# Attention on one core: a piece of V's products moved between a slot's two pairs of score products

## The reference, cut to what matters

```python
b, s, e = x.shape                      # 8, 512, 256
h = rel_table.shape[1]                 # 16
scale = e ** (-0.5)
q = split_heads(x @ Wq)
k = split_heads(x @ Wk)
v = split_heads(x @ Wv)
attn = jnp.einsum('bhqd,bhkd->bhqk', q, k) * scale
attn = jax.nn.softmax(attn, axis=-1)
attn = attn + bias[None]               # from rel_table
out = jnp.einsum('bhqk,bhkd->bhqd', attn, v)
out = out.transpose(0, 2, 1, 3).reshape(b, s, e)
mu = jnp.mean(out, axis=-1, keepdims=True)
var = jnp.var(out, axis=-1, keepdims=True)
out = (out - mu) / jnp.sqrt(var + EPS) * gamma + beta
```

## Time and profile before

| | us |
|---|---|
| runs shown | 1941.26, 1942.33, 1943.03 (median 1942.33) |
| profiled execution, its own time | 1946.43 |
| its span | 1944.7 |
| the attention loop in it (first to last transposed score product) | 862.8 to 1256.5 |

### The profile page before, as it was taken

One profiled execution on the slowest core, in us unless ns is written; L12 is line 12 of the kernel. 1 busy time (PEld: TensorE's weight loads), 2 busy tenths in 40 slices (PEclk: granted clock), 3 DMA queues, 4 the chain that ended last, 5 costly groups with the idle time before them and its releaser, 6 DMA issues. The chain is left out here.

```text
span 1944.7 us, 33241 instructions
## 1 busy us (share of the span) xinstructions
PE 1649.3 (85%) x9891; PEld 1115.5 (57%) x9892; DVE 1146.3 (59%) x1949; ACT 1080.2 (56%) x2236; POOL 659.6 (34%) x624
## 2 busy tenths in 40 slices
PE   4999999561599689899999999945999999999990
PEld 1433343260499656444444444433999999999990
DVE  6999998388411174358999999366233333333325
ACT  6888987540133234127788888625455555555554
POOL 0000000030266331211233333211576777777750
PEclk9999999775699889989999999985999999999995
DMA  5000000134122196603333434069344444444417
GB/s 179 1 0 1 0 1 0 47 103 157 33 67 64 47 336 234 111 1 78 78 100 100 100 100 111 24 211 335 53 70 71 70 69 71 65 68 70 69 21 259
DMA packets 145735, 173.67 MB, mean 89 GB/s; under 512 B 29139, under 2 KB 110430, under 8 KB 145504
## 3 DMA queue, kind: packets, MB, share of 16 engines
q1 hardware_dynamic: 104160, 128.29, 21.7%
q0 software_dynamic: 33248, 43.71, 12.7%
q10 hardware_dynamic: 8224, 0.39, 0.2%
HBM read 111.50 MB, written 66.19 MB: 91 GB/s over the span
## 5 line engine op out<-in xcount | busy, mean ns | idle before, releaser
L1359 PEld LDWEIGHTS f_ht_ps<-f_XT,f_WS 128*128 128x128 f32 x2912 | 358.6, 195 | 15.1 <-DVE f_WS L1452 2.6
L1359 PE MATMUL f_ht_ps<-f_XT,f_WS 128*128 128x128 f32 x2912 | 361.7, 278 | 3.0 <-ACT f_XT L1400 3.0
L1367 PE MATMUL f_y_ps<-W,f_HT 128*128 x1456 | 344.3, 380 | 0.0
L1325 POOL DMA_INDIRECT moe<-f_Y,TOK x182 | 276.9, 1521 | 185.3 <-ACT f_Y L1425 142.2
L2187 DVE TENSOR_REDUCE att_MX<-att_s_ps 128x2 f32<-128x1024 f32 x256 | 304.3, 1215 | 53.6 <-PE att_s_ps L1951 53.4
L2152 ACT ACTIVATE att_PT<-att_st_ps 128x512 f32<-128x512 f32 x512 | 278.7, 594 | 69.8 <-PE att_st_ps L1976 59.6
L1367 PEld LDWEIGHTS f_y_ps<-W,f_HT 128*128 128x128 f32 x1456 | 263.0, 191 | 28.2
L1452 DVE COPY f_WS<-W 128x1024 f32 x182 | 134.0, 737 | 205.0 <-PE f_ht_ps L1359 124.8
L1316 POOL DMA_INDIRECT XG<-x,TOK x182 | 191.1, 1050 | 178.6 <-issue 108.5
L1460 DVE TENSOR_TENSOR f_Y<-f_y_ps,f_B 128x256 f32<-128x256 f32 x143 | 60.7, 424 | 296.4 <-PE f_y_ps L1367 296.4
L303 PE MATMUL rec_ring<-rec_XC,rec_W 128*128 128x512 f32 x384 | 182.9, 630 | 49.7 <-DVE rec_XC L353 21.1
(11 more groups left out here) (291 smaller groups left out, 2191.3 us busy)
## 6 DMA issues: line engine op xcount, KB each, us to landing
W<-in_w SPq DMA_DIRECT2D x48, 512.0 KB, 10.0
att_Q<-qk_pairs SPq DMA_DIRECT2D x192, 64.0 KB, 2.8
att_K<-qk_pairs SPq DMA_DIRECT2D x192, 64.0 KB, 2.9
qk_pairs<-prj_HI SPq DMA_DIRECT2D x16, 512.0 KB, 3.8
qk_pairs<-prj_LO SPq DMA_DIRECT2D x16, 512.0 KB, 5.1
hidden<-in_xT SPq DMA_DIRECT2D x8, 512.0 KB, 7.7
x<-n_Y SPq DMA_DIRECT2D x8, 512.0 KB, 3.0
prj_X<-x SPq DMA_DIRECT2D x8, 512.0 KB, 8.8
```

Source lines behind the costliest of these rows:

```text
L1325: nc.gpsimd.indirect_dma_start(out=outs[n % len(outs)], out_offset=bass.IndirectOffsetOnAxis(ap=TOK[:, n:n + 1], axis=0), in_=Y[n % R][:], ...
L1359: mm = nc.tensor.matmul(ht_ps[r % 2][:, f * P:(f + 1) * P], WS[r % 2][:, at:at + P], XT[r % 2][:, c], start=(c == 0), stop=(c == DC - 1))
L1367: mm = nc.tensor.matmul(y_ps[r % 2][:], HT[r % 2][:, f], W2[:, bass.ds(e * W_EXPERT + f * D, D)], start=(f == 0), stop=(f == FC - 1))
```

## The change

In the slot, `sums` moves ahead of the second pair. Nothing is added or removed, and no wait is changed:

```diff
@@ -2059,11 +2059,11 @@
                     scores_T(i, slot, 0)
                     if i + LEAD < TWO:
                         scores(i + LEAD, slot, 1)
+                    if n >= 1:
+                        sums(n - 1, at)
                     if i + LEAD < TWO:
                         scores(i + LEAD, slot, 0)
                     scores_T(i, slot, 1)
-                    if n >= 1:
-                        sums(n - 1, at)
                     if p == 0 and slot == 1 and n + 1 < NGROUPS:
                         maxima(n + 1)
                     if p == 0 and slot == 3 and n >= 2:
```

## The result

The changed kernel takes 2011.35 us (median of four runs, 2009.39 to 2015.58) against 1942.68 before: a ratio of 1.0357, 95% interval 1.0340 to 1.0375. The direction was forecast, the size was not: +69 us in place of +40, outside the range of 1954 to 2002.

A forecast was written before the change was run, and what follows sets the result against it. PE was taken to set the pace, DVE having only 7% of air. +35.0 us for groups 2 to 29, 1.7 aggregates, 0.8 group 1 and 2 groups 30 and 31 made +39.5: median 1982, range 1954 to 2002.

The forecast's parts named there:

- PE's own work: PE's queue in each slot: plain slots still cost 1.22 us, slot 1 1.84 as before, slot 3 1.98, 0.06 less.
- the removed wait: Fourth product's weight load waiting for ACT's exponential: this wait, about 0.2 us in slot 5 and in slot 7, disappears.
- rival C: Slightly slower: only additional drain and load exposure in slots 1 and 3 count, 0.2 each, +12 us, 1954; chance 0.09.
- The first pair directly behind a second pair: PE at the slot's border: spacing without a wait taken as 0.34 us, bounds worth -8 and +17 us in total.
- ACT's side: Later second exponential delays the next slot's first; the old wait returns at the first product, two slots costing 2.65 us.
- DVE's side: Later reductions free buffers late: second product 0.12 us late in slot 6, 0.43 in slot 7; slots become 1.44 and 1.75.
- The group's border: V's piece 0 waits for slot 7's late exponential and ACT's copy, starting at 1.31; slot 0 2.21 us against 1.43.
- The sum of a group: Changes of slots 0 to 7 add to +1.25 us per group, +35.0 over the 28 groups 2 to 29.
- the 0 taken for the stall: POOL's residual holding DVE's CAST of slot 7 in six groups: difference taken as 0, bounds -1 and +1.2 us per group.
- Groups 1, 30 and 31 at full clock: Group 1 waits for exponentials but no copy, +0.8 us; groups 30 and 31 keep the border's wait, +2.
- the granted clock is 0.99, its level of 2.4 GHz: Clock read in the loop's stretch from 876.3 to 1228.3 us before the change; no forecast term changed it.
- PE's busy time in the loop: Sign to look for in the changed kernel's profile: the same or less, with more idle before it.

The follow-up runs named there:

- e12: Changed kernel with ACT's exponentials computing 256 of 512 columns from group 2 on; 2041.62 us, ratio 1.0490.
- e4: Changed kernel with DVE doing scale ahead of slot 4's reduction; four runs of 1984.35 to 2032.18 us, no ratio.
- e1: Changed kernel with V's piece between the pairs in slots 1 to 6 only, behind both pairs in slots 0 and 7; 1972.23 us, ratio 1.0161.
- e5: Changed kernel with ACT's copy of the sums between slot 7's two exponentials, not behind both; 1995.40 us, ratio 1.0257.
- e7: Changed kernel with six dummy transposes in slot 0's idle spot, plus eight small products per slot of group 0; 1988.50 us, ratio 1.0223.
- e8: Kernel before the change, with eight added products of 128 columns in each slot of group 0; 1944.24 us, ratio 1.0002.
- e3: Changed kernel with six dummy transposes on PE between slot 0's first pair and V's piece; 1986.08 us, ratio 1.0220.
- e14: Changed kernel with 256-column exponentials from group 2 on and six dummy transposes in slot 0's idle spot; 1980.91 us, ratio 1.0194.
- e10: Kernel before the change, with ACT copying the sums twice before releasing PE, except in the last three groups; 1953.26 us, ratio 1.0052.
- e13: Kernel before the change, with ACT copying the sums three times before releasing PE, except in the last three groups; 1974.12 us, ratio 1.0161.

## Why the prediction was wrong, by its own steps

**PE's own work and the removed wait**: right but for slot 2. Plain slots that nothing delays are 1.32 to 1.33, the fourth product no longer waits in full-clock slots, and in slots 1 and 3 nothing of rival C's 0.2 is seen (1.84 and 1.90, against 1.86 and 2.05 before). The first pair directly behind a second pair, which no row had shown, starts 0.34 later where nothing holds it; the value taken was right. Slot 2 is 0.11 longer than the 1.22 I gave it: its first product is not loaded ahead (it follows the maxima), which I had counted in slot 4 and forgot here. Slot 3 is 0.08 shorter than I gave it, as its first product is loaded ahead.

**ACT's side**: right. Slot 5 is 1.37 against 1.33, and 1.22 with short exponentials (e12): the wait did come back as one of the first product.

**DVE's side**: right. Slots 6 and 7 are 1.43 and 1.76 against 1.44 and 1.75, and e4 shows that scale between two reductions is the cause in slot 7. For slot 6, which e4 left at 1.43, the cause is the trace's releaser (DVE's reduction); no run tests it.

**The group's border**: right in mechanism, 0.13 too small. V's piece starts at 1.45 of slot 0, not 1.31: from the copy's end to its first matmul 0.14 pass (1050.86 to 1051.00), where I had taken 0.04, which is 0.10 of it. e1 and e5 show that slot 7's late exponential and the copy behind it make the wait.

**The sum of a group**: 1.37 as a mean, against 1.25 and the aggregates' 0.06: 38 against 37 us for groups 2 to 29, right. Groups with the aggregates grew by 1.67 (forecast 1.54), those with the residual by 1.12 (1.25 with the 0 taken for the stall).

**Groups 1, 30 and 31 at full clock**: nearly right. Where both orders run group 1 at 2.4 GHz, it takes 11.87 (e7) against 11.17 (e8), +0.70 for a forecast of +0.8. Groups 30 and 31 take 30.8 us at full clock (e3) against 27.7, +3.1 for a forecast of +2. With groups 2 to 29 that makes 42 us for the order alone, and the forecast had 39.5.

**What failed** is the step "the granted clock is 0.99, its level of 2.4 GHz": I kept it, and so a price of nothing for the clock, for a kernel in which I forecast an idle spot of about 1 us per group and two smaller ones. None of my terms nor rivals had the clock. In its place the profile shows 88 us of the loop at 1.2 GHz, against 17 before, and some 25 of the 67 us by which the loop grew are the price: 3.3 in group 1 (4.0 less the order's 0.7), 13.2 in groups 27 and 28, and 8.5 in groups 30 and 31 (11.6 less 3.1). Two pairs of runs show that it is the clock: e3, whose slots are the same, lost 25 of the 69 us by keeping PE busy, and the same fill took 61 us from e12 (e14). e3, which keeps 2.4 GHz from group 2 on, is the run to hold my sum against: 1986, 4 above it.

One of my signs failed too: PE's busy time in the loop was to be the same or less, and rose from 384.7 to 426.2 us. A product that takes 0.49 to 0.50 at 2.4 GHz takes 0.79 at 1.2. Not all of it is the clock: by the stretches of 330 us at full clock PE is busy for 12.4 us per group, against 11.9 before.

What a low stretch costs comes from the changed kernel: groups 27 and 28 lose 13.2 us over 37.5 at 1.2 GHz, 0.35 for each. A plain slot takes 2.13 there, with PE hardly idle (below, the second pairs of two slots in a row):

```profile
1239.85 0.79 PE L1951 MATMUL att_s_ps<-att_K,att_Q 48*128 48x512 f32 x1
...
1241.98 0.79 PE L1951 MATMUL att_s_ps<-att_K,att_Q 48*128 48x512 f32 x1
```

Open stays what exactly starts a fall and what ends it. In the changed kernel the clock fell at the start of group 27, but group 14 has the same idle spots as group 26 (1.05 and 0.31), and nothing happens behind it. e4 and e10 have idle spots of one size and differ. And the changed order stayed at 1.2 GHz for 37.5 us with PE busy 96% of the time, where the old order mostly returned within 3.5 us (e13). The fill adds work and takes idle time away at once; no run separates the two.

## What to carry to other kernels

When a producer moves behind other work in its queue, follow the latest result through every consumer's queue to the next wait on a buffer, first of all at a group's border, where two or three waits stand in series; that walk over one group, with spacings from the trace, was right to 0.14 us in every slot. Then ask what PE does in the new waits: here idle spots of 0.6 to 1.1 us per group, in a loop that had kept its 2.4 GHz, added some 25 us to the order's 42, and the bill differed from run to run. Dummy products in the idle spot are a cheap test for that: if the slots stay as they are and the time falls, it was the clock.

## What the runs showed of the hardware

- Less work can be slower: exponentials of half the length gave shorter slots and +30 us, by 195 us at 1.2 GHz in place of 88.
- One kernel differs by 48 us from run to run (e4, 1984 to 2032), the longer runs at the lower mean clock (0.911 against 0.882); with the idle spot filled the spread is 8 us or less (e3, 1983.9 to 1991.5; e14, 1980.5 to 1982.2).
- A PE idle spot once per 13 us can matter: 1.1 us at the border, with the old order (e13), came with falls of the clock, 0.61 (e10) with none; but 0.62 in the changed order (e4) came with one of 51 us, so that no limit on the spot follows from these runs.
